# Two row normalisations placed inside a routed feed-forward and inside the copy in front of the SAGE products

## What is computed

```
xn = layernorm(x)                                   # already in place when the feed-forward starts
out = sum over the 2 chosen experts of w_e * (gelu(xn @ W1_e + b1_e) @ W2_e + b2_e)
x  = x + (layernorm(out + xn) * gamma + beta)       # first normalisation of the change
x' = layernorm(x)                                   # second normalisation of the change
h_self, h_neigh = x' @ W_self, x' @ W_neigh
x  = x + h_self + mean over in-edges of top32(h_neigh)[src]
```

## Time and profile before

| | us |
|---|---|
| median of 3 runs | 6043.5 (6042.69 to 6044.06) |
| the profiled execution, its own time | 6044.03 |
| its span, first to last instruction | 6042.2 |
| routed feed-forward | 3516 to 3827 |
| ln_ffn and ln_x2 | 3827 to 3911 |
| SAGE products | 3911 to 4107 |

### The profile page before, as it was taken

The page is one execution under the profiler, slowest core; times in us unless marked ns, Lnnn a source line. Parts: engine busy times, 40 slices in busy tenths (PEclk is TensorE's granted clock), DMA queues, the critical chain, the costliest instruction groups (busy, mean ns, idle before and its releaser), DMA issues. The chain is left out here.

```text
span 6042.2 us, 94692 instructions
## 1 busy us (share of the span) xinstructions
PE 4482.7 (74%) x23232; PEld 3406.8 (56%) x23437; DVE 3914.2 (65%) x7196; ACT 2030.0 (34%) x4756; POOL 2834.4 (47%) x2751
## 2 busy tenths in 40 slices
PE   0779999999589999999859769364555555356996
PEld 0656666666476666666649769353334333334553
DVE  6678888888668888888666656795444444742332
ACT  0145555555315555555433323320000000223332
POOL 0077777775027777777300010006777777153332
PEclk6899999999799999999979889697777777558998
DMA  6466666665346666666420030012333333133333
GB/s 93 160 197 200 190 192 189 191 192 154 95 145 201 196 191 189 192 190 191 126 67 0 0 109 0 6 37 88 104 104 104 104 104 104 46 123 85 54 54 82
DMA packets 357897, 732.26 MB, mean 121 GB/s; under 512 B 73235, under 2 KB 205225, under 8 KB 357377
## 3 DMA queue, kind: packets, MB, share of 16 engines
q0 software_dynamic: 194912, 575.52, 33.9%
q1 hardware_dynamic: 156372, 143.87, 8.6%
q10 hardware_dynamic: 6350, 9.60, 0.5%
HBM read 627.96 MB, written 107.19 MB: 122 GB/s over the span
## 5 line engine op out<-in xcount | busy, mean ns | idle before, releaser
L1009 POOL DMA_INDIRECT rows_a<-kv_scratch,att_idx x848 | 862.5, 1017 | 887.7 <-ACT att_idx L1046 642.7
L752 POOL DMA_INDIRECT rows_a<-k_scratch,sage_sum_idx x832 | 795.7, 956 | 855.9 <-issue 851.1
L1009 POOL DMA_INDIRECT rows_c<-kv_scratch,att_idx x816 | 877.9, 1076 | 268.5 <-issue 242.2
L1467 PE MATMUL ps<-rows_a 128*128 128x258 f32 x1664 | 607.0, 529 | 470.3 <-DMA rows_a<-k_scratch,sage_sum_idx 305.8
L1147 PE MATMUL ps<-attention_rows_b,att_work 128*128 x3328 | 847.8, 395 | 52.5 <-DVE att_work L1255 36.5
L1066 ACT ACTIVATE attention_rows_b<-ps x1664 | 649.3, 390 | 589.0 <-PE ps L1161 409.7
L1467 PEld LDWEIGHTS ps<-rows_a 128*128 128x128 f32 x1664 | 417.3, 262 | 659.7 <-DVE sage_rows_b L1445 413.0
L1445 DVE TENSOR_TENSOR sage_rows_b<-sage_rows_b,ps 128x258 f32 x832 | 353.1, 424 | 560.9 <-PE ps L1467 365.8
L1147 PEld LDWEIGHTS ps<-attention_rows_b,att_work 128*128 128x128 f32 x3328 | 596.4, 191 | 166.7 <-issue 92.1
L1161 PE MATMUL ps<-rows_a,att_work 128*128 128x264 f32 x1696 | 515.3, 430 | 62.9 <-issue 51.8
L1161 PE MATMUL ps<-rows_c,att_work 128*128 128x264 f32 x1632 | 504.6, 429 | 36.3 <-issue 29.8
(11 more groups left out here) (402 smaller groups left out, 9335.6 us busy)
## 6 DMA issues: line engine op xcount, KB each, us to landing
kv_scratch<-rows_c SPq DMA_DIRECT2D x100, 256.0 KB
slot_in<-rows_c SPq DMA_DIRECT2D x1, 13674.0 KB
rows_a<-slot_in SPq DMA_DIRECT2D x106, 129.0 KB, 2.1
rows_a<-kv_scratch,att_idx POOLq DMA_INDIRECT x848
rows_a<-k_scratch,sage_sum_idx POOLq DMA_INDIRECT x832, 2.8
rows_c<-kv_scratch,att_idx POOLq DMA_INDIRECT x816
h_scratch<-rows_a SPq DMA_DIRECT2D x2, 6400.0 KB
rows_a<-h_scratch SPq DMA_DIRECT2D x50, 256.0 KB
```

What stands on the lines that cost most here:

```text
L752: pool.indirect_dma_start(ring[:, slot, 0:D], None, table, bass.IndirectOffsetOnAxis(ap=idx[:, slot:slot + 1], axis=0)).then_inc(landed[sl ...
L1009: pool.indirect_dma_start(r.halves[h][:, u, 0:KV], None, c.kv_dram[:, :], bass.IndirectOffsetOnAxis(ap=idx[:, slot:slot + 1], axis=0)).the ...
L1467: mm = pe.matmul(c.ps[:, to:to + nw], s_buf[:, q, u, :], rhs, start=True, stop=True)
```

## The change

`ffn` takes a new argument `norm`. With it the 25 groups are written out one by one on TensorE, ScalarE and VectorE (`each_group`), and a `NormTail` does the first normalisation in chunks of four groups. VectorE makes a chunk's variances behind its last group's statistics and its scales two groups later, ScalarE takes the square root in between and normalises the tiles of a group seven groups behind its own, and Pool, so far idle, multiplies by gamma, adds beta and adds the rows to `rows_c`, two tiles to an instruction. Ten groups behind, VectorE takes the statistics of the new `rows_c`. What has not been reached after group 24 follows there. The second normalisation has no stage either: `sage_products` makes the 50 scales at its start, and ScalarE's staging copy becomes an Identity with scale and bias for each tile, read from `rows_c`. The two calls of `layer_norm` go.

```diff
+def each_group(eng, body):
+    for g in range(GROUPS2):
+        body(g, g % 2, min(2, GROUPS2 - 1 - g))
+
+class NormTail:
+    CHUNK = 4
+    ROOT_LAG, APPLY_LAG = 2, 7
...
+    def variances(self, v, do, k):
+        c, (a, b) = self.c, self.cols(k)
+        v.wait_ge(self.taken, b)
...
+        do(v.tensor_tensor(mean, st[:, 1, :], st[:, 4, :], ALU.add))
...
+        do(v.tensor_scalar(rstd, rstd, 1.0 / D, LN_EPS, ALU.mult, ALU.add))
+        v.sem_inc(self.var_ready, 1)
+
+    def scales(self, v, do, k):
+        c, (a, b) = self.c, self.cols(k)
+        v.wait_ge(self.rooted, k + 1)
+        do(v.reciprocal(c.rstd[:, a:b], c.rstd[:, a:b]))
+        do(v.scalar_tensor_tensor(c.nbias[:, a:b], c.mean[:, a:b], -1.0, c.rstd[:, a:b], ALU.mult, ALU.mult))
+        v.sem_inc(self.scaled, 1)
+
+    def root(self, a, k):
+        lo, hi = self.cols(k)
+        a.wait_ge(self.var_ready, k + 1)
+        a.activation(self.c.rstd[:, lo:hi], self.c.rstd[:, lo:hi], ACT.Sqrt).then_inc(self.rooted, 1)
+
+    def apply(self, a, g):
+        a.wait_ge(self.scaled, g // self.CHUNK + 1)
+        for t in (2 * g, 2 * g + 1):
+            rows = self.c.rows_a[:, t * D:(t + 1) * D]
+            a.activation(rows, rows, ACT.Identity, bias=self.c.nbias[:, t:t + 1],
+                         scale=self.c.rstd[:, t:t + 1]).then_inc(self.normed, 1)
+
+    def vector_after(self, v, do, g):
+        if g % self.CHUNK == self.CHUNK - 1 or g == GROUPS2 - 1:
+            self.variances(v, do, g // self.CHUNK)
+        k = (g - self.CHUNK + 1 - self.ROOT_LAG) // self.CHUNK
+        if (g - self.CHUNK + 1 - self.ROOT_LAG) % self.CHUNK == 0 and k >= 0:
+            self.scales(v, do, k)
+        if g == GROUPS2 - 1:
...
+                    self.scales(v, do, k)
+
+    def scalar_after(self, a, g):
+        k = (g - self.CHUNK + 1 - self.ROOT_LAG) // self.CHUNK
+        if (g - self.CHUNK + 1 - self.ROOT_LAG) % self.CHUNK == 0 and k >= 0:
+            self.root(a, k)
+        if g >= self.APPLY_LAG:
+            self.apply(a, g - self.APPLY_LAG)
+        if g == GROUPS2 - 1:
...
+                    self.root(a, k)
+            for late in range(g - self.APPLY_LAG + 1, GROUPS2):
+                self.apply(a, late)
+
+    def gain_and_shift(self, pool):
+        pool.wait_ge(self.loaded, 32)
+        do = Chain(pool, self.made)
+        for g in range(GROUPS2):
...
+            pool.wait_ge(self.normed, 2 * g + 2)
+            do(pool.tensor_tensor(rows, rows, bc(self.gb.unsqueeze(1), shape), ALU.mult))
+            do(pool.tensor_tensor(rows, rows, bc(self.bb.unsqueeze(1), shape), ALU.add))
+            if self.add_to is not None:
+                to = rows3(self.add_to)[:, 2 * g:2 * g + 2, :]
+                do(pool.tensor_tensor(to, to, rows, ALU.add))
+            pool.sem_inc(self.affine, 1)
...
@@ ffn @@
+            tail = NormTail(c, s, name, taken, room_gb[:, 0:D], room_gb[:, D:2 * D], c.rows_c)
...
+                    if tail is not None:
+                        tail.load(sp, gamma, beta)
...
+                    if tail is not None:
+                        tail.scalar_after(a, g)
-                groups_ahead(a, body)
+                over_groups(a, body)
...
-                groups_ahead(pe, body)
+                over_groups(pe, body)
...
-                groups_ahead(v, body)
+                    if tail is not None:
+                        tail.vector_after(v, tail_do, g)
+                        if g >= LATER:
+                            next_stats(g - LATER)
+
+                def next_stats(g):
+                    v.wait_ge(tail.affine, g + 1)
+                    for t in (2 * g, 2 * g + 1):
+                        row_stats(v, c, c.rows_c, t, again)
+                LATER = 10
...
+                over_groups(v, body)
                 v.wait_ge(taken, NT)
+                if tail is not None:
+                    for g in range(GROUPS2 - LATER, GROUPS2):
+                        next_stats(g)
+                    v.wait_ge(again, NT)
@@ sage_products @@
-                f.stage(a, 0, 0)
+                a.wait_ge(var_ready, 1)
+                a.activation(c.rstd[:, :], c.rstd[:, :], ACT.Sqrt).then_inc(rooted, 1)
+                a.wait_ge(scaled, 1)
+
+                def stage(g, parity):
+                    a.wait_ge(f.turned, g + 1)
+                    for u in range(2):
+                        t = g * 2 + u
+                        a.activation(rows[parity][:, u * D:(u + 1) * D], c.rows_c[:, bass.ds(t * D, D)], ACT.Identity,
+                                     bias=c.nbias[:, bass.ds(t, 1)], scale=c.rstd[:, bass.ds(t, 1)]).then_inc(f.staged, 1)
+                stage(0, 0)
...
+                row_scales(v, c, Chain(v, scale_step), var_ready, rooted, scaled)
@@ build @@
-            ffn(c, room, ACT.Gelu, c.rows_a, "moe_all", clear_slots=True)
+            ffn(c, room, ACT.Gelu, c.rows_a, "moe_all", True, (work[:, 0:2 * D], L0_ffn_gamma, L0_ffn_beta))
...
-            layer_norm(c, c.rows_a, c.rows_a, "ln_ffn", True, L0_ffn_gamma, L0_ffn_beta, c.rows_c)
-            layer_norm(c, c.rows_c, c.rows_a, "ln_x2")
```

More of the change, by code:

```diff
@@ L1477, in row_bc, with __init__, load, cols @@
     return ap.rearrange("(a n) -> a n", a=1).broadcast_to([P, ap.shape[0]])
+def each_group(eng, body):
[4 more added lines that the diff above has]
+    ROOT_LAG, APPLY_LAG = 2, 7
+    def __init__(self, c, s, name, taken, gb, bb, add_to=None):
+        self.c, self.taken, self.gb, self.bb, self.add_to = c, taken, gb, bb, add_to
+        self.chunks = -(-GROUPS2 // self.CHUNK)
+        self.loaded, self.step, self.var_ready, self.rooted, self.scaled, self.normed, self.made, self.affine = (
+            s.sem(f"{name}_{n}") for n in ("gain", "tail_step", "var", "root", "scaled", "normed", "made", "affine"))
+    def load(self, sp, gamma, beta):
+        sp.dma_start(self.gb, row_bc(gamma)).then_inc(self.loaded, 16)
+        sp.dma_start(self.bb, row_bc(beta)).then_inc(self.loaded, 16)
+    def cols(self, k):
+        return k * self.CHUNK * 2, min((k + 1) * self.CHUNK * 2, NT)
+    def variances(self, v, do, k):
+        c, (a, b) = self.c, self.cols(k)
+        v.wait_ge(self.taken, b)
+        st = c.stats[:, a * 6:b * 6].rearrange("p (t k) -> p k t", k=6)
+        mean, rstd, tmp = c.mean[:, a:b], c.rstd[:, a:b], c.small[:, a:b]
+        do(v.tensor_tensor(mean, st[:, 1, :], st[:, 4, :], ALU.add))
+        do(v.tensor_scalar(mean, mean, 0.5, None, ALU.mult))
+        do(v.tensor_tensor(tmp, st[:, 1, :], st[:, 4, :], ALU.subtract))
+        do(v.tensor_tensor(tmp, tmp, tmp, ALU.mult))
+        do(v.tensor_tensor(rstd, st[:, 2, :], st[:, 5, :], ALU.add))
+        do(v.scalar_tensor_tensor(rstd, tmp, D / 4.0, rstd, ALU.mult, ALU.add))
+        do(v.tensor_scalar(rstd, rstd, 1.0 / D, LN_EPS, ALU.mult, ALU.add))
[23 more added lines that the diff above has]
+        if g == GROUPS2 - 1:
+            for k in range(self.chunks):
+                if k * self.CHUNK + self.CHUNK - 1 + self.ROOT_LAG > g:
+                    self.scales(v, do, k)
[6 more added lines that the diff above has]
+        if g == GROUPS2 - 1:
+            for k in range(self.chunks):
+                if k * self.CHUNK + self.CHUNK - 1 + self.ROOT_LAG > g:
+                    self.root(a, k)
[5 more added lines that the diff above has]
+        for g in range(GROUPS2):
+            shape = [P, 2, D]
+            rows = rows3(self.c.rows_a)[:, 2 * g:2 * g + 2, :]
+            pool.wait_ge(self.normed, 2 * g + 2)
[5 more added lines that the diff above has]
+            pool.sem_inc(self.affine, 1)
@@ L1626, in ffn, with _ @@
         hid_high, hid_split = sem("hid_high"), sem("hid_split")
+        over_groups, tail, again = groups_ahead, None, sem("next_stats")
+        if norm is not None:
+            room_gb, gamma, beta = norm
+            over_groups = each_group
+            tail = NormTail(c, s, name, taken, room_gb[:, 0:D], room_gb[:, D:2 * D], c.rows_c)
         with nc.Block() as block:
+            if tail is not None:
+                @block.gpsimd
+                def _(pool):
+                    tail.gain_and_shift(pool)
             if clear_slots:
@@ L1754, in body @@
                         row_stats(v, c, target, g * 2 + u, taken)
-                groups_ahead(v, body)
+                    if tail is not None:
[7 more added lines that the diff above has]
+                LATER = 10
+                tail_do = None if tail is None else Chain(v, tail.step)
+                over_groups(v, body)
                 v.wait_ge(taken, NT)
+                if tail is not None:
+                    for g in range(GROUPS2 - LATER, GROUPS2):
+                        next_stats(g)
+                    v.wait_ge(again, NT)
 def mlp_weights(c, room, w1, b1, w2, b2):
@@ L1933, in sage_products @@
         stored, buf_free, gate = [sem(f"stored{u}") for u in range(4)], sem("buf_free"), sem("gate")
-        f = Front(c, s, "sage", rows, rows_t, c.rows_a)
```

(14 more changed lines are left out.)

3 lines of the change are left out of this document (1 added, 2 removed).

## The result

The changed kernel takes 5996.45 us (median of 4 runs, 5994.23 to 5997.66) against 6043.78 us on the same chip (4 runs, 6042.69 to 6047.74): a ratio of 0.9921, 95% interval 0.9907 to 0.9934. Faster, as forecast, and 0.5 us from the predicted 5996. The profiled execution took 5994.23 us, its span is 5992.5.

What follows compares the result with a forecast made beforehand. No engine was above 74% busy, so a chain of barrier-parted stages, with the normalisations wholly on the path, bounds the kernel. Terms -52.6 + 0.9 + 0.5 + 4.0 = -47.2 us gave a median of 5996 us, range 5980 to 6028.

Steps and rivals of the forecast that it cites:

- Tail: From the last feed-forward statistics to the SAGE block: 31.9 us against 84.5, so 52.6 us less.
- SAGE prologue: Start of the SAGE block: the 50 scales now precede the first staging, so TensorE starts later, +0.9 us.
- Table loads: ScalarE's loads around square roots between Gelus: +0.5 us; as a rival, all ten in full, 6008 us, chance 0.10.
- Unrolled code: Feed-forward groups written out: fetched ahead, no cost; as a rival, TensorE waits for each packet, 6026 us, chance 0.08.
- rival of 30: Written-out feed-forward: TensorE waits 1.2 us for an instruction packet in each of 25 groups, 30 us; chance 0.08.
- Pool beside VectorE: Feed-forward groups 7, 11, 15, 19: Pool holds up VectorE's hidden splits and TensorE stalls, 1.0 us each, +4.0 us.
- The sign of being wrong that did come: Middle of the feed-forward loop: VectorE's hidden splits longer than 0.43 and 0.69 us would make the forecast wrong.
- The slower rival: Groups 7 to 23: Pool holds VectorE up until it becomes the bound; 6063 us at 2.0 us an instruction; chance 0.07.

Runs made afterwards that it cites:

- e3: The changed kernel with the tail's seven square roots replaced by a copy of the same shape, so no table loads between Gelus; 6005.43 us (one run).
- e1: The kernel before with only the 25 feed-forward groups written out on TensorE, ScalarE and VectorE; 6054.88 us against 6058.41 for the kernel before.
- e5: The changed kernel with Pool waiting until all 50 tiles are normalised, behind the feed-forward; 6080.17 us against 6046.35 for the kernel before.
- e10: The changed kernel with beta added five times more on Pool, eight instructions a group; 6132.17 us against 6057.29 for the kernel before.
- e9: The changed kernel with scales of groups 16 to 19 applied early, VectorE taking groups 20 to 24, Pool adding beta early for 16 to 24; ratio 0.9897.
- e11: As e9, but Pool keeps groups 20 and 21 and VectorE works on three tiles at a time; 5986.56 us, ratio 0.9893 to the kernel before.
- e4: The changed kernel with a fourth Pool instruction a group, adding beta twice; 6015.24 us (one run).

## Why the prediction was right

By its own steps, in the profiled execution:
- *Tail*, predicted 31.9, measured 33.3: in front of Pool 2.74 (predicted 2.9), 21 instructions 28.67 (27.3), statistics 0.84 (0.8), barrier 1.03 (0.9). Pool's instruction, the one unknown price, was put at 1.2 us between 0.57 and 1.47, by the number of passes over IOTA's rate; it takes 1.26. With the Trainium skill's ratio of 1.96 (GPSIMD Engine Reference, Performance versus the Vector engine) and VectorE's 0.69 us the estimate was 1.36; the ratio measured here is 1.26 / 0.69 = 1.83.
- *SAGE prologue*, predicted +0.9: the first transposition comes 4.34 us behind the issue (4.5 predicted; 3.66 before), but VectorE's first add comes 0.30 us earlier than before and the stage is 0.24 longer, so -0.1. The stretch from issue to first add ranges from 12.3 to 14.4 us in the table, so a term of 0.9 can't be told from it.
- *Table loads*, predicted +0.5: e3 shows nothing beyond the scatter of the loop.
- *Unrolled code*, predicted free with a rival of 30: e1 shows 0.1.
- *Pool beside VectorE*, predicted +4.0 from 1.0 in each of four groups (7, 11, 15, 19): e5 shows 1.7. The mechanism and the place were right: the splits of the hidden values are held where the variances have made VectorE late, and TensorE gets the row split late behind groups 11, 15 and 19. The size was too large, since Pool meets only two such instructions there (2.1 us, not 3.6), only one behind group 7, and none in the other groups, so TensorE loses 0.6 three times.
- Together 1.87 in the loop, 0.25 in the last statistics, -51.23 in the tail and -0.1 in SAGE: -49.2 against the predicted -47.2, and -47.3 between the medians.
- That the median came within 0.5 us is luck. The tail turned out 1.4 us longer and the last statistics 0.25, the loop 2.6 and SAGE 1.0 less than their terms, which cancel in part, and the two profiled executions differ by 49.8 us where the medians differ by 47.3.

The sign of being wrong that did come, longer splits in the middle of the loop, was badly chosen: the sum's own +4.0 supposes just that.

The slower rival named the right mechanism with the wrong condition. It let all three Pool instructions of every group hold VectorE for their whole length, 17 x (3 x 1.26 - 2.85) = 16 us in the loop where e5 shows 1.7, and it asked how long a Pool instruction is. In e10 Pool's instruction is no longer than in the changed kernel (1.26 us alone), but there are eight, and the kernel is 75 us slower than before: what decides is how many of VectorE's casts and instructions with two SBUF inputs Pool meets in front of what TensorE waits for.

## What to carry to other kernels

Work moved beside a stage that another engine paces costs next to nothing as long as it fits the idle time: here 84.5 us on the path became 33.3, and the 1.9 us given back in the loop are small against that. What is left is the tail behind the last group, so look first at how many groups lag there and which engine works them off: sharing them by engine and moving what doesn't depend on the last group forward gave 14 us more (the stretches of e9 and e11; 17.6 in e11's time). Before giving Pool elementwise work in SBUF, list which VectorE instructions it will meet: those with two SBUF inputs, the fast casts and short serial chains of them were held up here by up to 1.1 us for each Pool instruction; statistics and adds from PSUM were not.

## What the runs showed of the hardware that I had not expected

- A Pool add over 128x512 and a VectorE one, meeting all the time, take 1.67 us a pair: VectorE's grows by 0.95 to 1.1 us, Pool's by 0.32. That fits exclusion of everything but the two starts (0.69 + 1.26 - 0.16 - 0.12 = 1.67, an estimate from rows of short instructions); Pool instructions of another length were not tried beside VectorE.
- The delay doesn't depend on the length of VectorE's instruction: 0.17 us became 1.15 on 8 columns, 0.43 became 1.52 on 512. It is smaller only where VectorE's instruction starts late in Pool's (the b2 add of e4, 0.23 to 0.43 us).
- Ten table loads of 1.28 us between Gelus, on whose results TensorE depends, took nothing that shows (306.93 us without them, 306.73 with).
- With Pool at eight instructions a group a quarter of the loop's loss of 70.9 us was not waiting but slower matmuls behind the waits, 0.21 us apart instead of 0.12; the granted clock of that stretch fell from 1.00 to 0.88 on average. Behind the three waits of 0.33 us in the changed kernel it stayed at 1.00.
